# Value matmuls moved behind the first score matmul of a step, and the order of the 64-row matmuls changed

## The reference, cut to what matters

```
x = L0_attn_x                                     # 4 x 1024 x 128, f32
x = x + layernorm(attn0(layernorm(x)))            # 16 heads of 8, ALiBi bias, causal
x = x + layernorm(ffn(layernorm(x)))
# ffn(u): u = u + layernorm1(attn1(u))            # 16 heads of 8, not causal
#         u = u + layernorm2(moe(u))              # 8 experts, top 2, 512 wide
# attention: softmax(q k^T / sqrt(8) [+ bias, mask]) v, then an output projection
```

## Time and profile before

| | |
|---|---|
| median of 3 runs | 1684.19 us (1681.83 to 1684.7) |
| the profiled execution, its own time | 1682.8 us |
| its span, first to last instruction | 1681.1 us |
| PE / DVE / ACT / POOL busy, share of the span | 85% / 77% / 65% / 32% |
| mean granted TensorE clock | 0.915 |

### The profile page before, as it was taken

How to read it: one execution, slowest core, us unless ns; L and a number is a source line. 1 busy time by engine, 2 the same in 40 slices (tenths; PEclk the granted TensorE clock), 3 DMA queues, 4 the chain that set the end, 5 groups by cost and what they waited for, 6 DMA issues and landing times. The chain is left out here.

```text
span 1681.1 us, 27511 instructions
## 1 busy us (share of the span) xinstructions
PE 1424.7 (85%) x9143; PEld 712.0 (42%) x9143; DVE 1296.1 (77%) x2638; ACT 1097.2 (65%) x2256; POOL 536.7 (32%) x624
## 2 busy tenths in 40 slices
PE   3389999999999999999999999999999831999400
PEld 3145555555555443443344333433343221788300
DVE  4378888889888989999999999999998023655355
ACT  4036677677676557778777787778777820999444
POOL 5114544534525322340122312323141406000274
PEclk9569999999999989999999999999999965999855
DMA  6402241322322222133221122102210124788322
GB/s 168 145 28 73 84 133 50 112 81 65 102 89 72 74 71 66 43 90 91 69 65 53 52 64 78 54 32 75 61 46 33 57 78 131 224 247 248 110 63 69
DMA packets 105822, 148.96 MB, mean 89 GB/s; under 512 B 13236, under 2 KB 63164, under 8 KB 105680
## 3 DMA queue, kind: packets, MB, share of 16 engines
q1 hardware_dynamic: 100348, 138.18, 28.0%
q0 software_dynamic: 4096, 8.40, 1.7%
q10 hardware_dynamic: 1236, 0.62, 0.2%
HBM read 78.70 MB, written 67.13 MB: 87 GB/s over the span
## 5 line engine op out<-in xcount | busy, mean ns | idle before, releaser
L474 ACT ACTIVATE at_probs<-at_b 128x512 f32<-128x512 f32 (+3 forms) x1792 | 866.3, 557 | 380.8 <-PE at_b L411 376.2
L589 DVE TENSOR_REDUCE at_mx<-at_a 128x1 f32<-128x512 f32 (+3 forms) x1664 | 992.0, 661 | 89.5 <-PE at_a L393 28.3
L411 PE MATMUL at_b<-fq,km 64*128 64x512 f32 (+3 forms) x1792 | 669.1, 439 | 16.7 <-ACT at_probs L474 13.3
L388 PE MATMUL at_a<-km,fq 64*128 64x512 f32 (+2 forms) x1664 | 549.9, 453 | 46.3 <-DMA fq<-rest 35.2
L411 PEld LDWEIGHTS at_b<-fq,km 64*128 64x128 f32 x1792 | 295.9, 187 | 405.0 <-ACT at_probs L474 340.5
L424 PE MATMUL at_pv<-at_probs,at_vst 128*32 128x512 f32 (+3 forms) x3584 | 442.0, 566 | 0.0
L388 PEld LDWEIGHTS at_a<-km,fq 64*128 64x128 f32 x1664 | 273.8, 191 | 146.2 <-DVE at_mx L589 82.9
L747 POOL TENSOR_SCALAR_AFFINE_SELECT at_probs<-at_probs 128x512 f32<-128x512 f32 x128 | 81.5, 636 | 284.0 <-ACT at_probs L474 283.1
L1653 POOL DMA_INDIRECT t_got<-expert_out,t_out_pos x64 | 63.5, 993 | 171.4 <-issue 171.4
L424 PEld LDWEIGHTS at_pv<-at_probs,at_vst 128*32 128x32 f32 x3584 | 71.0, 108 | 104.2 <-issue 49.2
L393 PE MATMUL at_a<-half_mask,half_ident 64*128 64x128 bf16 (+1 forms) x768 | 108.7, 251 | 0.0
(11 more groups left out here) (237 smaller groups left out, 1254.2 us busy)
## 6 DMA issues: line engine op xcount, KB each, us to landing
t_w<-w_parts SPq DMA_DIRECT2D x46, 512.0 KB, 4.4
sums<-at_osb SPq DMA_DIRECT2D x64, 256.0 KB, 2.0
fq<-query SPq DMA_DIRECT2D x128, 96.0 KB
km<-key SPq DMA_DIRECT2D x128, 96.0 KB
w_parts<-at_parts SPq DMA_DIRECT2D x16, 512.0 KB, 3.0
query<-at_q_hi SPq DMA_DIRECT2D x24, 256.0 KB, 3.1
key<-at_k_hi SPq DMA_DIRECT2D x24, 256.0 KB, 3.7
t_x_tok<-expert_rows SPq DMA_DIRECT2D x23, 256.0 KB, 4.8
```

Of the source, the lines that this page charges most:

```text
L388: mm = pe.matmul(scores, fq[g][rows_, qt * P:(qt + 1) * P], km[g][rows_, first:first + k, kh * HALF:kh * HALF + w], start=True, stop=not d ...
L411: pe.matmul(b_bank[k % B_BANKS][:, 0:w], km[g][rows_, j % 2, kt * P:(kt + 1) * P], fq[g][rows_, q0:q0 + w], start=True, stop=True).then_in ...
L474: act.activation(probs[t % PROBS][:, j, 0:w], b_bank[k % B_BANKS][:, 0:w], ACT.Exp).then_inc(exp_done, 1)
L589: dve.tensor_reduce(mx[:, kh, qt, heads[0]:heads[0] + k], bank_of(step)[:, 0:k * w].rearrange("p (k w) -> p k w", k=k), AX.X, ALU.max).the ...
```

## The change

In `program()` the value matmul `pv` of quad i+1 and its `oev` move from the end of loop step i to behind its first `b`. The step's `a` move back by one `b`. `m`, `mtr` and the row steps stay at the end of the step. The chunk list of a wide tile changes from heads 0, 2, 1, 3 to 0, 2, 3, 1.

The diff also brings `paired` plans, in which one `a` step fills two banks and one reduction reads both. Both plans are made with `paired=False`, so in this kernel each `a` step still has one matmul (with its masks), one bank and one reduction, and the four banks still go round one by one; they are now halves of two wide tensors.

```
-                for j in (0, 2) if per == 2 else (0, 2, 1, 3):
-                    self.chunks.append((qt, kh, list(range(j, j + per)), n))
+                if paired:
+                    self.chunks += [(qt, kh, (tuple(range(j, j + per)), tuple(range(j + 2, j + 2 + per))), n)
+                                    for j in range(0, 2, per)]
+                else:
+                    self.chunks += [(qt, kh, (tuple(range(j, j + per)),), n)
+                                    for j in ((0, 2) if per == 2 else (0, 2, 3, 1))]
...
-PLANS = (Plan(True), Plan(False))
+PLANS = (Plan(True, False), Plan(False, False))
...
-            out += bs[:1] + ass[:half] + bs[1:2] + ass[half:] + bs[2:]
+            out += bs[:1]
+            at, q = (s, i + 1) if i + 1 < p.nq else (s + 1, 0)
+            if at < SLOTS:
+                out.append(("pv", at, q))
+                if q in plan_of(at).half_end:
+                    out.append(("oev", at, plan_of(at).half_end.index(q)))
+            out += bs[1:2] + ass[:half] + bs[2:3] + ass[half:] + bs[3:]
             if s + 1 < SLOTS:
                 if i == p.m_step:
                     out.append(("m", s + 1, 0))
                 if i == p.mt_step:
                     out.append(("mtr", s + 1, 0))
-            at, q = (s, i + 1) if i + 1 < p.nq else (s + 1, 0)
-            if at < SLOTS:
-                out.append(("pv", at, q))
-                if q in plan_of(at).half_end:
-                    out.append(("oev", at, plan_of(at).half_end.index(q)))
             out += rows.get((s, i), [])
...
-        a_bank = [bank(f"a{i}") for i in range(A_BANKS)]
+        a_pair = [ctx.enter_context(nc.psum_tensor(f"at_a{i}", [P, 2, HALF], F32)) for i in range(A_PAIRS)]
```

More of the change, by code:

```diff
@@ L52, in slopes @@
     return [start * start ** i for i in range(H)]
-A_BANKS = 4
+A_PAIRS = 2
 B_BANKS = 3
@@ L75, with __init__ @@
 class Plan:
-    def __init__(self, causal):
+    def __init__(self, causal, paired):
         self.causal = causal
@@ L296, in attend @@
                 series[s, n] = len(series) + 1
-        ring = [step for step in steps if step[0] in RING]
-        place = {step: k for k, step in enumerate(ring)}
+        place, users_before, users = {}, {}, [None] * (2 * A_PAIRS)
+        spot = 0
+        for step in steps:
+            if step[0] in RING:
+                width = len(plan_of(step[1]).chunks[step[2]][2]) if step[0] == "a" else 1
+                spot += spot % width
+                place[step] = spot % len(users)
+                taken = range(place[step], place[step] + width)
+                users_before[step] = [u for k, u in enumerate(users) if k in taken and u is not None]
+                for k in taken:
+                    users[k] = step
+                spot += width
         row_order = [(what,) + n for what, s, n in steps if what in ENGINE_OF]
@@ L335, in bank_of, with pair_with @@
         def bank_of(step):
-            return a_bank[place[step] % A_BANKS]
+            return pair_with(step)[:, place[step] % 2, :]
+        def pair_with(step):
+            return a_pair[place[step] // 2]
         def block_of(x, n):
@@ L357, in bank_free @@
             def bank_free(step):
[L359 to L369, removed]
+                for what, s, n in users_before[step]:
+                    if what == "a":
+                        done(pe, a_read, "a", s, n)
+                    elif what == "mtr":
+                        done(pe, m_read, "mtr", s, n)
+                    else:
+                        reader = dict(project="y", turn="turned", values_mm="values", q="q_out", k="k_out", logits="gate",
+                                      rank="pos")[what]
+                        after(pe, reader, n)
             for step in steps:
@@ L382, in _ @@
                     diagonal = plan_of(s).causal and kh * HALF + w == (qt + 1) * P
[L384 to L395, removed]
+                    parts = list(enumerate(heads))
+                    for at, js in parts[::-1] if n % 2 else parts:
+                        k = len(js)
+                        bank_ = misc if len(heads) == 1 else pair_with(step)[:, at, :]
+                        scores = bank_[:, 0:k * w].rearrange("p (k w) -> p k w", k=k)
+                        rows_ = slice(PAIR * (js[0] // 2), PAIR * (js[0] // 2 + 1))
+                        first = js[0] % 2
+                        mm = pe.matmul(scores, fq[g][rows_, qt * P:(qt + 1) * P],
+                                       km[g][rows_, first:first + k, kh * HALF:kh * HALF + w],
+                                       start=True, stop=not diagonal)
+                        if diagonal:
+                            for i in range(2):
+                                mm = pe.matmul(scores[:, :, w - P:w], half_ident[rows_, i, :],
+                                               half_mask[rows_, i, None, :].broadcast_to([PAIR, k, P]),
+                                               start=False, stop=(i == 1))
                     mm.then_inc(a_made, 1)
@@ L587, in _ @@
                             dve.wait_ge(m_step, 2 * s - 1)
[L588 to L591, removed]
+                    k, j = len(heads[0]), heads[0][0]
+                    if len(heads) == 1:
+                        dve.tensor_reduce(mx[:, kh, qt, j:j + k],
+                                          bank_of(step)[:, 0:k * w].rearrange("p (k w) -> p k w", k=k),
+                                          AX.X, ALU.max).then_inc(a_read, 1)
+                    elif k == 1:
+                        dve.tensor_reduce(mx[:, kh, qt, j:j + 3:2], pair_with(step)[:, :, 0:w], AX.X,
+                                          ALU.max).then_inc(a_read, 1)
+                    else:
+                        dve.tensor_reduce(mx[:, kh, qt, :].rearrange("p (h k) -> p h k", k=k),
+                                          pair_with(step)[:, :, 0:k * w].rearrange("p h (k w) -> p h k w", k=k), AX.X,
+                                          ALU.max).then_inc(a_read, 1)
                 elif what == "m":
```

## The result

| | before | after |
|---|---|---|
| median | 1683.4 us (1681.83 to 1684.7, 4 runs) | 1695.08 us (1693.92 to 1695.46, 4 runs) |
| ratio, 95% interval | | 1.0069 [1.0051, 1.0086] |
| profiled execution, own time / span | 1682.8 / 1681.1 us | 1695.21 / 1693.5 us |

The forecast was 1687 in a range of 1672 to 1702, with slower as the likeliest sign. The sign and the wide range held. The time lies above the forecast's own range of 1681 to 1693, and the sum behind the forecast did not hold: two of its terms were wrong in opposite directions, the one for `mtr` by some 15 us, the one for the causal slots by some 12.

What follows compares the result with a forecast made beforehand. A 2.60 us latency chain over PE and ScalarE (`b`, exponential, next `b`, `pv`) was taken as the bound. Terms 0 - 8 + 2.5 + 8.8 + 2.7, then -1 and -2, gave +3 us: 1687, range 1672 to 1702.

Steps and rivals of the forecast that it cites:

- slower as the likeliest sign: Whole kernel: chance of slower 0.39, against 0.30 for faster and 0.31 for same.
- Plain loop: Plain full steps: the loop `b`, exponential, next `b`, `pv` stays at 2.60 us under the new order, 0.
- The rival of a gain in every step: Full slots: pairs of halves shorten every step towards VectorE's 2.47 us, -33 us, 1651; chance 0.12.
- Causal slots: Causal slots: same terms added in another order, sum over a slot unchanged, 0, with 3 us either way.
- Relief of VectorE: Where VectorE is late: it starts some 0.2 us earlier in 42 stretches of full and causal slots, -8 us.
- Bank waits: Row steps beside four `a`: the bank is 0.1 us late in some 25 of them, +2.5 us.
- Late inputs: Row steps waiting for GpSimd: 3 projections, 7 q and 4 others get their input late, +8.8 us.
- `mtr`, +2.7: Full slots: the stall stays in four, `b` 0's 0.42 comes after it, +1.7; ten others wait 0.1 more, +1.
- rival 3: Row steps: the drain around them is not covered, a third of 77 x 0.42 is +11 us, 1698; chance 0.20.
- the sum of +3: Whole kernel: all terms together, +3 us on the profiled 1682.8, 1685.8, or 1687 as a median.

Runs made afterwards that it cites:

- the two short exponentials: Changed kernel, from slot 18 on one exponential per quad handling 256 of 512 columns: `b` 1's 1669.0 us, `b` 2's 1695.17 us, one execution each.
- The last run: Changed kernel with the `a` of causal slots' first five steps spread 2, 3, 4, 4, 3 instead of 3, 4, 3, 3, 3: 1689.94 us.

## Why the prediction held, and where its sum was wrong

**Plain loop, 0: right.** It is 2.60 before and after, and the two short exponentials show which exponential it hangs on. The rival of a gain in every step is out, and with it, for this kernel, the gain that the Trainium skill, "TensorE: Matmul & The Clock Gate", Part 3, would lead one to hope for: alternating halves brought the first reduction forward from 0.76 to 0.57 and the step not at all.

**Causal slots, "0, with 0.2 us a slot either way": the mis-sized term.** It measured +1.27 us in each of slots 4, 8 and 12, and slots 0 to 14 together, late inputs included, +16.6. Of that, 1.4 goes with the clock: in slot 3 it was granted at 0.50 from 220.3 to 223.7 us, and the slot took 34.33 where slots 1 and 2 took 32.9. The step that failed is "the same terms are added in another order, so the sum over a slot is the same". It holds for the loop alone. But a step ends with the later of the loop and VectorE's banks, and the move changed which steps are short while the `a` stayed on their step numbers. The last run shows this for 0.75 of the 1.27. The other 0.5 lies in t = 5 to 7, around `mtr` (7.45 before, 7.95 now), and in t = 8 to 0 (10.29 and 10.82), with t = 1 to 4 now 0.5 better than before. Its cause stays open: in the run with all `a` spread anew, t = 8 with two `a` instead of four was no shorter (2.26 and 2.20), so the number of maxima in that step does not explain it.

**Relief of VectorE, -8: did not come.** The statistics step was to fall from 3.35 to 3.15; it is 3.34. A step with five `a` takes 2.97 in both. In the trace the statistics start 1.01 us ahead of `pv` (863.07 and 864.08), as before (1.00): there VectorE seems to work from its own queue, so that an `a` that is ready sooner only waits longer. No run tested this by itself.

**Bank waits, +2.5: right as far as seen.** A transposing step took 3.32 instead of 3.19, logits 4.16 instead of 4.03: 0.13, where 0.1 was put.

**Late inputs, +8.8: right in kind and place.** The projection step grew by 0.85 (put: 0.9), the q of slot 6 by 0.47 (0.7), the q of slots 0 to 3 by 1.00. Moving q and k a step later brought back 4.6 us in slots 0 to 14.

**`mtr`, +2.7, "the stall stays": wrong.** The stall went, in all four slots: -12.9 us in those slots; in slots 16 and 20 a step with a reciprocal gave 0.34 of it. With the stall went the stretches behind it in which the granted clock was 0.50 (from 648.8, 833.1, 1020.9 and 1205.2 us before). The prediction had the length of the join, 1.21, but did not ask what made 1.21 of an operation that elsewhere takes 0.19, and it did not see the cast's 1.18. It was GpSimd, with `heads_t` and the operation behind it, and the earlier `oev` let `heads_in` go sooner; the prediction had moved `oev` without looking at what stands behind it in SyncE's queue. The old order with `heads_in` ahead of `oev` shows that an earlier `heads_in` by itself is worth nearly all of it, 11.8 us in these slots.

**Drain around row steps, rival 3: its time was near, its mechanism was not seen.** 1698 would have needed a third of the row steps to pay 0.42 each; those read without a late input pay 0.13. The rule of the Trainium skill, "TensorEngine Tiling (Array Packing)", Key Properties, still fits the 0.42 between the last 64-row load and `pv`; around the row steps it stayed covered.

**Not foreseen: slot 15, +4.0.** Its five steps with six to eight `a` (t = 0 to 4 before, 1 to 5 after, 36 `a` each) took 31.75 instead of 28.13 us. Their windows, before and after:

```profile
571.84:599.97 28.13, 26.39 (x109) 12.09 (x108) 24.33 (x45) 10.11 (x22) 7.18 (x9) 0.76 0.18 48
```

```profile
590.05:621.80 31.75, 30.06 (x110) 13.45 (x108) 24.44 (x46) 10.60 (x22) 7.17 (x9) 0.62 0.10 27
```

VectorE does the same work; the mean granted clock is 0.62 instead of 0.76. After, it is 0.50 without a break from 595.8 to 619.7 us; before, it was 0.50 only from 577.1 to 580.5 and from 587.4 to 597.6 us. Ahead of the fall at 595.8 TensorE waits for VectorE's reductions, one `a` each 0.6 us. That the clock explains the +4.0 is likely and not shown, as no run took this apart.

So the sum of +3 became +12.4 by about +17 in causal slots 0 to 14 (of it some 5 for late q and k, 2.5 for three late projections, 6 for maxima in short steps, 1.4 for the clock in slot 3, the rest open), +4 in slot 15, -13 at four transposes of maxima, and +5 in the other full slots. Of this last, 2.1 lies in slots 26 and 30, where the granted clock is 0.50 for a stretch (from 1138.5 and 1295.5 us) that the kernel before does not have. That the time still fell into the range was in part luck: the stall that the prediction kept, and that went, paid for most of what it missed in the causal slots.

## What to carry to other kernels

A sum over steps is kept under a new order only if every step stays bound by the same thing; where steps differ in length, lay the side work out anew by the new lengths, and count it bank by bank. When an operation takes six times its usual length, look for what runs beside it on the other engines before taking its length as given: here one DMA, put ahead of another in an in-order list, was worth 0.65%. A DMA that is issued earlier in the program gains nothing while it stands behind one that waits.

## What the runs showed of the hardware

A VectorE join of 128x32 took 0.19 us with no GpSimd operation beside it and 1.21 us when a 1.28 us GpSimd operation had started 0.11 us before it. It ended (831.82) when that operation did (830.50 + 1.28 = 831.78), so it waited for it and did not share with it. The Trainium skill, "SBUF — State Buffer", Who interferes with whom, states this: a VectorE instruction with two SBUF inputs contends with a GpSimd instruction that reads SBUF, and the one that issued first blocks the other. The trace agrees here, and the old order with an earlier `heads_t` shows the other side, 0.19 us. The cast behind the join, which reads one tile, was held up in the same way: 1.18 instead of 0.19 us, ending at 833.03 with GpSimd's next operation (831.73 + 1.26 = 832.99).
